# A Mamba, int8 MLP and MoE layer on one core: scans 2 to 4 regrouped to 4 states x 32 channels

## The chip, the core and the metric

The kernel runs on one core of a Trainium2 chip. The metric is the device time in microseconds. The engines are called as in the profile: PE (TensorE matmuls; PEld its weight loads), DVE (VectorE), ACT (ScalarE), POOL (GpSimd) and SP, whose queue issues most of the DMAs.

## What is computed

Four sequences (batches) of 512 tokens x 512 features pass through three sublayers with residuals. The one that matters here is a Mamba mixer:

```python
xz = einsum('ed,bld->bel', in_proj_weight, hidden_states)       # x: 1024 channels, z: 1024
x = silu(depthwise_conv4(x))
dt, Bc, Cc = split(x_proj_weight @ x, [128, 16, 16])
delta = softplus(dt_proj_weight @ dt + dt_proj_bias)
def step(h, (d_t, B_t, C_t, u_t)):                              # h: 1024 channels x 16 states
    h = h * exp(d_t[..., None] * A) + (d_t * u_t)[..., None] * B_t[:, None, :]
    y = einsum('bdn,bn->bd', h, C_t)
y = (ys + u * D) * silu(z)
out = out_proj_weight @ y
```

Then comes an int8 MLP ("smooth quant": two linear layers whose operands are scaled, rounded and clipped) and a mixture of 16 experts, top 2, with a shared expert beside it. Everything is float32 except the integer matmuls.

## The kernel before

**Stages.** `first()` prepares batch 0, `scan_stage(0)` scans it. Then for b = 1, 2, 3: `between(b, b-1)` projects batch b and runs the MLP of batch b-1, and `scan_stage(b)` scans batch b while it runs the experts of batch b-1. `last(3)` and `scan_stage(4, False, True)` finish batch 3. The change touches the three stages with b > 0, and what prepares them. The profiled scan stage of b = 2 is taken as the example: its units run from 815 to 1073 us of the span.

**A unit.** A scan stage has 128 units c = 16 j + n: block j of 128 channels, state n. For one unit ACT makes the decay `exp(delta[:, j] * A[n])` into one of three PSUM banks (`decay`, line 942), DVE runs the scan over 512 tokens (`scan_unit`, line 1277) and multiplies by the row C[n] (`product`, line 1289), and PE adds the products of a block into the bank Y with the identity as weights (`nsum`, lines 1870, 1876, 1881; line 1880 adds u x D once a block). POOL makes the inputs delta x u x B for two units at a time (`chunk`, line 663), and `du_block` once a block (line 651). Of 8 units POOL also multiplies one by C (line 718, unit 7 of 8, `on_pool`) and adds the products of two unit pairs (line 715), so that PE has 3 matmuls for 4 units. B and C stand spread over all 128 partitions in the tiles BB and CB (16 rows each), loaded by `broadcast`.

**Order.** Each engine's program is a loop over the unit number p, with the other work hung in at fixed p: an expert visit v begins at VISIT_AT[v] (8 shared visits every 4 units from p = 4, 23 routed ones every 3 units from p = 38) with `gate_up` on PE (line 1946), the tanh on ACT at +3, two DVE steps at +4 and +5 (lines 1304, 1311) and `down` on PE at +7 (line 1967 shared, 1975 routed). Four units ahead of a routed visit PE transposes its rows (line 1922). The output projection (`mixer_part`, line 2072) stands at p = 107 to 126. Engines are in order, so a late step holds all that is behind it on its engine.

**Softplus.** delta is made in steps; those of blocks 4 to 7 (line 1266 on DVE, 644 on POOL, inverses at line 915 on ACT) lie at the beginning of the scan stage, around p = 1.

**SP's queue** is in order too: a wait in it holds every DMA behind it. `load_up(w)` (line 442, 512 KB) waits for the gate_up of visit w-2 and `load_down(w)` (line 451, 256 KB) for the down of visit w-3. The loop `load_experts` issues load_up(w+2) and load_down(w+3) for w = 0 to 7, then waits for the scattered rows, then issues for each routed visit its down weights, rows (line 461), the store of finished rows and its up weights.

## Time and profile before

| | us |
|---|---|
| median of 3 runs | 1689.95 (1688.96 to 1692.02) |
| span of the profiled execution | 1684.0 |
| what lies around the span | 6.0 (median less span) |
| PE busy | 1428.3 (85%) |
| DVE busy | 1344.6 (80%) |
| ACT busy | 801.0 (48%) |
| POOL busy | 1060.6 (63%) |
| mean DMA | 150 GB/s, 252.13 MB |

How to read it: an engine's busy time is the union of its instructions. Matmuls are pipelined, so PE's busy time says how often it had something in hand, and its real pace is read from the distance between starts. A float32 matmul is two records (x2), with a weight load before each. The timeline gives start, duration and, in brackets, the idle time before and who ended it.

### The profile page before, as it was taken

How to read it: one execution, taken by the hardware profiler on the slowest of the kernel's cores; microseconds unless marked ns; L12 is line 12 of the kernel's file. 1: busy time of each engine (PE TensorE's matmuls, PEld its weight loads, DVE VectorE, ACT ScalarE, POOL GpSimd, SP SyncE). 2: the span in 40 equal slices, each digit the busy share in tenths (PEclk: the TensorE clock that was granted, in tenths of full speed). 3: DMA queues.
4: the chain of work that ended last, by engine and by line, in shares of the span. 5: the costliest groups of instructions: out<-in, count | busy, mean ns of one | idle time of the engine just before them, and what ended most of it. 6: DMA issues, size and time to landing. Idle time of an engine off the chain costs nothing.

```text
span 1684.0 us, 19335 instructions
## 1 busy us (share of the span) xinstructions
PE 1428.3 (85%) x5368; PEld 809.6 (48%) x5376; DVE 1344.6 (80%) x2215; ACT 801.0 (48%) x1374; POOL 1060.6 (63%) x684
## 2 busy tenths in 40 slices
PE   7588679999599899999599899999599999836994
PEld 4233224444365565444265565444265665324783
DVE  4588999676899999786899999796899999784212
ACT  3666444246634565246634565245734565222141
POOL 0399898103999899402999899501999999522101
PEclk9899899999799999999799999999799999968997
DMA  3550001403446673613535674612534773700984
GB/s 119 220 187 25 1 0 38 135 28 116 192 138 184 208 237 123 212 38 105 228 118 188 207 234 142 212 38 102 231 113 153 233 235 130 250 25 20 350 334 140
DMA packets 94073, 252.13 MB, mean 150 GB/s; under 512 B 11024, under 2 KB 11152, under 8 KB 88848
## 3 DMA queue, kind: packets, MB, share of 16 engines
q1 hardware_dynamic: 86688, 229.93, 40.3%
q0 software_dynamic: 5120, 16.78, 3.1%
q10 hardware_dynamic: 2160, 4.19, 0.6%
q8 instruction: 44, 0.72, 0.2%
q14 instruction: 61, 0.50, 0.1%
HBM read 207.87 MB, written 42.99 MB: 149 GB/s over the span
## 4 chain that ended last, share of the span: by engine, by line
PE 54%; DVE 17%; issue 12%; ACT 8%; POOL 7%; DMA 1%; DVEq 0%; POOLq 0%; SPq 0%; ACTq 0%
PE bank L1946 10%; PE bank L1804 7%; DVE bank L1277 5%; PE bank L2072 5%; PE bank L1817 5%; PE bank L1876 4%; PE bank L1881 4%; POOL work L663 4%; PE bank L1975 3%; PE bank L1870 3%; PE bank L1967 2%; PE bank L1922 2%; DVE work L1289 2%; DVE pairs L1289 2%; PE bank L1845 2%
## 5 line engine op out<-in xcount | busy, mean ns | idle before, releaser
L663 POOL TENSOR_TENSOR work<-du,BB 128x1024 f32<-128x1024 f32 x255 | 598.8, 2357 | 5.2 <-DVE work L1553 4.4
L942 ACT ACTIVATE bank<-delta,A_sb 128x512 f32<-128x512 f32 x512 | 349.9, 690 | 460.7 <-DVE pairs L1289 246.2
L1277 DVE TENSOR_TENSOR_SCAN bank<-bank,work 128x512 f32<-128x512 f32 x432 | 522.6, 1219 | 7.8 <-POOL work L663 4.0
L1946 PEld LDWEIGHTS bank<-x3T,ew_up 128*128 128x128 f32 x1488 | 215.7, 193 | 72.5 <-issue 63.7
L1946 PE MATMUL bank<-x3T,ew_up 128*128 128x128 f32 (+1 forms) x1488 | 235.8, 304 | 5.2 <-issue 5.2
L1289 DVE TENSOR_TENSOR pairs<-bank,CB 128x512 f32<-128x512 f32 x240 | 161.0, 671 | 3.9 <-PE bank L1881 2.9
L608 POOL TENSOR_TENSOR col<-col,halfpow 128x4 f32<-128x4 f32 (+1 forms) x8 | 7.8, 973 | 208.9 <-DVE col L1429 208.9
L1876 PE MATMUL bank<-pairs,ident 128*128 128x512 f32 x160 | 91.9, 659 | 43.7 <-DVE pairs L1289 16.6
L1289 DVE TENSOR_TENSOR work<-bank,CB 128x512 f32<-128x512 f32 x192 | 128.3, 668 | 0.0
L1817 PE MATMUL bank<-xT,wst 128*128 128x512 f32 x256 | 118.8, 610 | 9.2 <-DVE ew_up L1266 7.4
L2072 PE MATMUL bank<-wst,zg 128*128 128x512 f32 x256 | 117.0, 593 | 0.9 <-DVE zg L1297 0.9
L1804 PE MATMUL bank<-xT,wst 128*128 128x512 f32 x256 | 114.4, 593 | 0.7 <-ACT xT L829 0.7
L1241 DVE SCALAR_TENSOR_TENSOR u<-etm,cw,u 128x512 f32<-128x512 f32 x96 | 72.2, 752 | 40.6 <-ACT u L849 38.3
L1304 DVE SCALAR_TENSOR_TENSOR etm<-etm,bank 128x128 f32<-128x128 f32 (+1 forms) x124 | 38.6, 311 | 80.5 <-ACT etm L995 80.5
L1876 PE MATMUL bank<-work,ident 128*128 128x512 f32 x160 | 83.5, 604 | 12.5 <-POOL work L718 10.2
L715 POOL TENSOR_TENSOR work<-work 128x512 f32<-128x512 f32 x48 | 60.7, 1266 | 45.5 <-DVE work L1289 45.3
L1975 PE MATMUL bank<-ew_dn,etm 128*128 128x512 f32 x138 | 73.2, 612 | 18.2 <-ACT x3T L1009 17.9
L718 POOL TENSOR_TENSOR work<-work,CB 128x512 f32<-128x512 f32 x64 | 81.3, 1271 | 10.9 <-DVE work L1277 10.9
L1881 PE MATMUL bank<-pairs,ident 128*128 128x512 f32 x160 | 86.7, 625 | 0.0
L848 ACT COPY etm<-bank 128x512 f32<-128x512 f32 x32 | 18.8, 587 | 140.7 <-PE bank L1804 140.7
L1277 DVE TENSOR_TENSOR_SCAN work<-bank,work 128x512 f32<-128x512 f32 x64 | 77.5, 1211 | 8.8 <-PE bank L1881 6.3
L1817 PEld LDWEIGHTS bank<-xT,wst 128*128 128x128 f32 x256 | 49.3, 195 | 72.6 <-issue 59.2
(259 smaller groups left out, 2493.4 us busy)
## 6 DMA issues: line engine op xcount, KB each, us to landing
ew_up<-in_exp_w SPq DMA_DIRECT2D x93, 512.0 KB, 3.7
ew_dn<-in_exp_w SPq DMA_DIRECT2D x93, 256.0 KB, 4.3
hm<-xs_dram SPq DMA_DIRECT2D x69, 256.0 KB, 4.6
ys_dram<-x3T SPq DMA_DIRECT2D x69, 256.0 KB, 4.6
wst<-in_w_in SPq DMA_DIRECT2D x64, 256.0 KB, 2.7
BB<-bc_dram SPq DMA_DIRECT2D x16, 1024.0 KB, 7.7
CB<-bc_dram SPq DMA_DIRECT2D x16, 1024.0 KB, 9.7
wst<-in_out_w SPq DMA_DIRECT2D x32, 256.0 KB, 3.0
```

The lines of the kernel that those rows point to most:

```text
L663: nc.gpsimd.tensor_tensor(dBu[:, k % CHUNK_SLOTS, :, :], du[:, j % 2:j % 2 + 1, :].broadcast_to([P, 2, T]), BB[:, n0:n0 + 2, :], ALU.mult) ...
L718: nc.gpsimd.tensor_tensor(hi, hi, CB[:, (2 * m + 1) % NS, :], ALU.mult).then_inc(S["pool_prod"], 1)
L942: nc.scalar.activation(R[q % RING][:, :], delta[:, j, :], ACT.Exp, scale=A_sb[:, j, n:n + 1]).then_inc(S["da_ready"], 1)
L1277: V.tensor_tensor_scan(prod[c % (2 * PAIR_SLOTS)] if on_pool(q) else R[q % RING][:, :], R[q % RING][:, :], dBu[:, c // 2 % CHUNK_SLOTS, c ...
L1289: V.tensor_tensor(prod[c % (2 * PAIR_SLOTS)], R[q % RING][:, :], CB[:, n, :], ALU.mult).then_inc(S["prod_done"], 1)
L1804: ins = mm(ps[:, :], wst[:, slot, k * P:(k + 1) * P], xT[:, k, :], start=(k == 0), stop=(k == KD - 1))
L1817: ins = mm(z_bank(a, m)[:, :], wst[:, slot, k * P:(k + 1) * P], xT[:, k, :], start=(k == 0), stop=(k == KD - 1))
L1876: mm(Y[:, :], ident[:], prod[2 * (m % PAIR_SLOTS)], start=(m % (NS // 2) == 0), stop=False)
L1881: mm(Y[:, :], ident[:], prod[2 * (m % PAIR_SLOTS) + 1], start=False, stop=(m % (NS // 2) == NS // 2 - 1)).then_inc(S["nsum_done"], 1)
L1946: ins = mm(gu_bank(v)[:, part * n:(part + 1) * n], w[:, part * D + k * P:part * D + (k + 1) * P], rhs, start=(k == 0), stop=(k == KD - 1))
L1975: mm(down_ps[1][:, :], eT[:, v % 2, 0:P], w, start=True, stop=True).then_inc(S["down_done"], 1)
L2072: ins = mm(acc[t][:, :], zg[:, k, t * P:(t + 1) * P], wst[:, W_POS["o", m, k] % W_RING, :], start=(k == 0), stop=(k == NBLK - 1))
```

## The change

In the scans of b = 1, 2, 3 a unit is no longer one state of 128 channels but 4 states of 32 channels: partition 32 s + i holds state s of a group and channel 32 q + i, with c = 16 j + 4 g + q (state group g, quarter q of the block's channels). Batch 0 stays as it was, with the states in another order in the weights.

- B and C need 4 tiles each (Brep, Crep, filled by `spread_rows`: 8 DMAs of 256 KB) and no longer 16.
- delta and delta x u of a block must stand four times, once for each state of a group. `replicate(b, j)` writes both to DRAM (2 stores of 256 KB), waits until these have landed, and loads them back into drep and durep in 8 DMAs of 256 KB. The decay reads drep, the chunk reads Brep and durep.
- The sum over the states of a partition group is made by PE: `quad_sum(g)` has four matmuls for four units, with a 128 x 32 matrix `fold` as weights, each into 32 partitions of Y (tile_position (0, 32 q)). The pair sums on POOL are gone.
- POOL makes 2 of 8 products with C (units 3 and 7), DVE 6; before it was 1 and 7.
- Products have 16 slots and no longer 8.
- The visits of the scan stages begin at p = 9, every 3.25 units for the shared ones and from p = 39 every 3 for the routed; the first down moves from p = 12 to 17. The router's steps move by 2 to 5 units, the scatters are at 2 a step. In the last stage all stays.
- The `lost` steps, products and subtractions of the softplus of blocks 4 to 7 move into the unit loop (DVE p = 0, 1 and 6, 7; POOL k = 7, 8), as do ACT's second row norm, inverses and the copies to x3T.
- The loads of the next MLP's weights change their place: guT and gu at the end of the stage wait for the last chunk and the last product.

```diff
+QUADS = UNITS // 4
+SLOTS = 16
+GROUPS = 4
+ROWS = P // GROUPS
...
+STAGE = Order(visits=tuple(9 + 13 * v // 4 for v in range(SHARED)) + tuple(39 + 3 * r for r in range(ROUTED)),
+              norm=1, inverses=3, x3=5, logits=7, logits_copy=9, route=10, rank=14, place=15, first_down=17,
+              gate_sums=10, gates=19, gate_weights=14, scatter=11, scatters=2)
...
+LOST_AT = {4: 0, 5: 0, 6: 1, 7: 1}
+ERROR_AT = {4: 6, 5: 6, 6: 7, 7: 7}
+LESS_AT = {4: 7, 5: 7, 6: 8, 7: 8}
...
-    return q % 8 in ((3, 7) if q < UNITS else (7,))
+    return q % 8 in (3, 7)
...
+REPLICATE_BEFORE = {j: min(i for i in range(3, ROUTED + 3) if STAGE.visits[SHARED + i - 3] >= NS * (j - 1))
+                    for j in range(4, NBLK)}
...
+            def replicate(b, j):
+
+                n = NBLK * (b - 1) + j
+                sp.wait_ge(S["delta_ready"], NBLK * b + j + 1)
+                sp.dma_start(rep_dram[j], delta[:, j, :]).then_inc(S["rep_out"], 16)
+                sp.wait_ge(S["du_ready"], NBLK * b + j + 1)
+                sp.dma_start(rep_dram[NBLK + j], du[:, j % 2, :]).then_inc(S["rep_out"], 16)
...
+                    sp.wait_ge(S["da_ready"], UNITS * b + NS * (j - 1))
+                    sp.wait_ge(S["dbu_ready"], PAIRS * b + NS // 2 * (j - 1))
+                sp.wait_ge(delta_in, replicas(b, j))
+                sp.wait_ge(du_in, replicas(b, j))
+                sp.wait_ge(S["rep_out"], 32 * (n + 1))
+                for src, dst, landed in ((rep_dram[NBLK + j], durep[j % 2], du_in), (rep_dram[j], drep[j % 2], delta_in)):
+                    for g in range(GROUPS):
+                        sp.dma_start(dst[g * ROWS:(g + 1) * ROWS, :, :],
+                                     src.rearrange("(q i) t -> i q t", q=GROUPS)).then_inc(landed, 16)
...
                     if w + DOWN_RING < SHARED:
                         load_down(be, w + DOWN_RING)
+                    if w == 3:
+                        replicate(be + 1, 2)
+                replicate(be + 1, 3)
                 sp.wait_ge(S["scattered"], 16 * 2 * TT * (be + 1))
...
                 for j in range(ROUTED + 6):
+                    for i in range(4, NBLK):
+                        if REPLICATE_BEFORE[i] == j:
+                            replicate(be + 1, i)
...
-                    broadcast(b, 0)
+                    spread_rows(b)
                     weights("z", b, 4, NBLK)
-                    wait(sp, "lin_ps", 2 * TT * b)
-                    broadcast(b, 1)
+                    replicate(b, 0)
+                    replicate(b, 1)
                     weights("o", b, 0, 4)
...
+                    nc.gpsimd.tensor_tensor(
+                        dBu[:, k % CHUNK_SLOTS, :, :], Brep[:, g:g + 1, :].broadcast_to([P, 2, T]),
+                        durep[j % 2][:, q0:q0 + 2, :], ALU.mult).then_inc(S["dbu_ready"], 1)
...
-                    for i in range(4):
+                    for i in range(2):
                         softplus_lost(a, i)
-                    softplus_less(a, 0)
-                    du_block(a, 0)
-                    chunk(a, 0)
-                    for i in range(1, 4):
                         softplus_less(a, i)
+                        du_block(a, i)
                 if m is not None:
                     norm(2 * m + 1)
                 if a is not None:
+                    chunk(a, 0)
+                    for i in range(2, 4):
+                        softplus_lost(a, i)
+                        softplus_less(a, i)
                     for i in range(4, 8):
                         softplus_sum(a, i)
...
+                src = delta[:, j, :] if b == 0 else drep[j % 2][:, n % GROUPS, :]
+                nc.scalar.activation(R[q % RING][:, :], src, ACT.Exp, scale=(A_first if b == 0 else A_sb)[:, j, n:n + 1]
...
-                for i in range(4, 8):
-                    lost(a, i)
...
+                def quad_sum(g):
...
+                    pe.wait_ge(S["prod_done"], dve_products(UNITS * b + 4 * g + 4))
+                    pe.wait_ge(S["pool_prod"], pool_products(UNITS * b + 4 * g + 4))
+                    if part == GROUPS - 1:
+                        pe.wait_ge(S["skip_ready"], NBLK * b + j + 1)
+                        mm(Y[:, :], skip_diag(b, j), u[:, j, :], start=False, stop=False)
+                    for q in range(GROUPS):
+                        ins = mm(Y[q * ROWS:(q + 1) * ROWS, :], fold[:], slot(b, 4 * g + q), start=(part == 0),
+                                 stop=(part == GROUPS - 1), tile_position=(0, q * ROWS))
+                    ins.then_inc(S["nsum_done"], 1)
```

## Rows read from the trace of the kernel before

**Rows 1.** Windows of stage 2: window, length, busy time (instructions), PEclk, DMA share, GB/s

```profile
core 0: us, PE busy (x) PEld busy (x) DVE busy (x) ACT busy (x) POOL busy (x), PEclk, DMA share, GB/s
828.00:890.00 62.00, 56.75 (x203) 36.69 (x204) 60.49 (x107) 23.41 (x41) 59.77 (x40) 0.97 0.31 107
890.00:1030.00 140.00, 129.87 (x631) 85.30 (x630) 135.84 (x200) 78.17 (x146) 128.77 (x75) 0.99 0.70 215
1030.00:1082.00 52.00, 51.58 (x145) 24.47 (x144) 43.91 (x57) 20.28 (x35) 41.44 (x27) 1.00 0.48 167
```

**Rows 2.** Timeline of DVE in mid-stage, back to back: start, us, engine, line, operation

```profile
914.19 1.22 DVE L1277 TENSOR_TENSOR_SCAN bank<-bank,work 128x512 f32<-128x512 f32 x1
915.32 0.67 DVE L1289 TENSOR_TENSOR pairs<-bank,CB 128x512 f32<-128x512 f32 x1
915.91 1.22 DVE L1277 TENSOR_TENSOR_SCAN bank<-bank,work 128x512 f32<-128x512 f32 x1
```

**Rows 3.** Timeline of DVE: units 0 and 1, softplus, then units 2, 8, 32, 40, 104

```profile
815.37 2.33 DVE L1277 TENSOR_TENSOR_SCAN bank<-bank,work 128x512 f32<-128x512 f32 x2
820.27 6.79 DVE L1266 TENSOR_TENSOR work<-pairs,work 128x512 f32<-128x512 f32 x4 [2.57 <-ACT work L915]
827.80 1.22 DVE L1277 TENSOR_TENSOR_SCAN bank<-bank,work 128x512 f32<-128x512 f32 x1
...
840.13 1.22 DVE L1277 TENSOR_TENSOR_SCAN bank<-bank,work 128x512 f32<-128x512 f32 x1
...
890.18 1.23 DVE L1277 TENSOR_TENSOR_SCAN bank<-bank,work 128x512 f32<-128x512 f32 x1 [0.60 <-POOL work L663]
...
906.21 2.34 DVE L1277 TENSOR_TENSOR_SCAN bank<-bank,work 128x512 f32<-128x512 f32 x2
...
1029.78 2.34 DVE L1277 TENSOR_TENSOR_SCAN bank<-bank,work 128x512 f32<-128x512 f32 x2
```

**Rows 4.** Timeline of PE in the shared visits, back to back

```profile
880.11 1.02 PE L1870 MATMUL bank<-work,ident 128*128 128x512 f32 x2
880.97 1.88 PE L1967 MATMUL bank<-ew_dn,etm 128*128 128x512 f32 x4
882.69 1.02 PE L1876 MATMUL bank<-work,ident 128*128 128x512 f32 x2
...
884.41 3.62 PE L1946 MATMUL bank<-x3T,ew_up 128*128 128x256 f32 x16
887.86 1.02 PE L1870 MATMUL bank<-pairs,ident 128*128 128x512 f32 x2
```

**Rows 5.** Timeline of PE: a matmul with 32-column weights between ones with 128

```profile
748.29 1.04 PE L1844 MATMUL bank<-u,xpw 128*32 128x512 f32 x2
749.27 1.12 PE L1845 MATMUL bank<-u,xpw 128*128 128x512 f32 x2
750.23 3.60 PE L1817 MATMUL bank<-xT,wst 128*128 128x512 f32 x8
```

**Rows 6.** Costliest groups of the page: busy us, mean ns

```profile
L718 POOL TENSOR_TENSOR work<-work,CB 128x512 f32<-128x512 f32 x64 | 81.3, 1271 | 10.9 <-DVE work L1277 10.9
```

**Rows 7.** Timeline of SP: one issue of a broadcast, one of expert weights (visit 7)

```profile
803.20 0.44 SPq L423 DMA_DIRECT2D BB<-bc_dram  x1
...
883.26 0.46 SPq L442 DMA_DIRECT2D ew_up<-in_exp_w  x1
```

**Rows 8.** Chain that ended last: start, us, a 256 KB load, a 256 KB store

```profile
893.98 2.84 DMA hm<-xs_dram
...
1663.19 2.01 DMA ys_dram<-zg
```

**Rows 9.** DMA view of 800 to 812 us, all 16 engines busy

```profile
DMA packets 1098, 4.93 MB, mean 411 GB/s; under 512 B 112, under 2 KB 112, under 8 KB 624
```

**Rows 10.** Timelines around the start and the end of stage 2: POOL, ACT, PE

```profile
804.70 1.27 POOL L651 TENSOR_TENSOR du<-delta,u 128x512 f32<-128x512 f32 x1
810.01 1.90 ACT L942 ACTIVATE bank<-delta,A_sb 128x512 f32<-128x512 f32 x3
...
1081.36 3.60 PE L1804 MATMUL bank<-xT,wst 128*128 128x512 f32 x8
```

More of the change, by code:

```diff
@@ L9 @@
 from contextlib import ExitStack
+from dataclasses import dataclass
 import numpy as np
@@ L299, in rows_bank, with slot @@
             return bank[1] if r < 2 else bank[0]
+        def slot(b, c):
+            return prod[c % (2 * PAIR_SLOTS)] if b == 0 else slots[c % SLOTS]
         def width(v):
```

364 lines of the change are left out of this document (232 added, 132 removed).

## Prediction

> **What bounds the kernel now.** I read the chain that ended last first: PE has 54% of it, DVE 17%. Then the stages: the timeline shows three scan stages of equal shape, 382 us apart, so I work out stage 2 and take it three times. In windows of that stage [rows 1] three engines are full at once: from 828 to 890 us DVE has 60.5 of 62 us, POOL 59.8, PE 56.8; to 1030 us DVE has 135.8 of 140; in the last 52 us PE has 51.6 and DVE only 43.9. The timelines say who leads. In mid-stage DVE's starts touch: 1.13 us from a scan to what follows, 0.59 from a product to the next scan [rows 2]. A group of 8 units costs DVE 8 x 1.13 + 7 x 0.59 = 13.2 us before any expert work, and 123.6 us pass from unit 40 to unit 104 [rows 3], 15.4 us for 8. In the shared visits PE touches too: 0.86 us for a matmul of the sum, 1.72 for a down, 3.45 for a gate_up [rows 4]; 8 units hold two visits (10.3) and six sums (5.2), 15.5 us. At the end the last product is done at about 1072.3, but PE begins the next stage at 1081.4 [rows 10]: there it is 9 us behind DVE. So a microsecond taken from DVE counts between units 40 and 104, one taken from PE in the head and in the tail.
>
> **The parts.** The sum is made against the span of 1684.0; the median is 6.0 above it, and I add the change to the median.
>
> (a) *DVE.* One product of 8 goes to POOL: 16 a stage x 0.59 = 9.4 us [rows 2]. Units 40 to 104 are half of them: **-4.7**. In the head PE and the loads set the pace (below), in the tail PE does: nothing there. POOL loses 32 pair sums and gains 16 products, all of about 1.27 us [rows 6]: 20 us less work, so it no longer holds DVE.
>
> (b) *PE's sum.* Three matmuls for four units (3 x 0.86 = 2.58 us) become four with 32 columns of weights. A float32 matmul is two records of 0.43 us. The trace has 32-column matmuls among wide ones: start to start 0.98 and then 0.96 us where 0.86 is the rate [rows 5], so entering and leaving costs 0.11 each, 0.22 a group. What it doesn't have is four of them into four different column groups. The bounds: all in a row, 4 x 0.86 + 0.22 = 3.66 us; all four at once, 0.86 + 0.22 = 1.08. I take the middle case: starts keep their order and the second record of a matmul needs the columns of its first, so only the second record of one and the first of the next can overlap: 5 records, 2.15 + 0.22 = **2.37** a group. Against 2.58 that is 0.21 less for each of six groups in the tail: **-1.3**. In the middle PE isn't the limit: 2.67 visits (3.1 us each, 8.3), two groups (4.7) and a skip matmul (0.4) are 13.4 us for 8 units, under DVE's 13.9.
>
> (c) *The way into the stage.* Scan 0 now starts at 815.4 [rows 3]. The decay at 810.0 [rows 10] will need drep: du of block 0 is done at about 802 (its instruction is at 804.7 now [rows 10], and two of the four 1.25 us `lost` steps ahead of it go). Two stores land 0.8 + 2.5 us later (2.01 for one [rows 8]), eight issues take 8 x 0.45 us [rows 7], and 2.1 MB at 411 GB/s [rows 9] take 5.1 us after 2.2 us of latency (2.84 less the bytes of rows 8). That gives 813 to 814 for drep and 815.5 for scan 0: nothing lost. Scan 2 stands at 827.8 behind a wait and the 6.8 us of softplus products [rows 3]. After, chunk 1 is queued on POOL behind four sums (about 826.5), and the softplus products come at p = 6 and 7, under no wait; six units x 1.57 (13.2 less 0.59, by 8) and 5.4 to 6.8 us give 841 to 843 for unit 8, now 840.1: **+1**, up to +3.
>
> (d) *SP's queue in the shared visits.* This is the largest term. `replicate(b, 2)` stands after load_down(6), which waits for the down of visit 3, at p = 25. PE needs from visit 0 (845 us) five gate_ups, four downs, four groups and the ranks: 17.3 + 6.9 + 9.5 + 2.7, so 881; DVE alone would be there at 876. I take 880. Stores to 883.3, eight issues to 887, and only then load_up(6), whose 0.5 MB lies behind 2.1 MB: 883.3 + 2.2 + 2.6 MB / 411 GB/s = 892. Its gate_up stands at p = 28; the tanh at p = 31 gives it one unit of grace, to 887. Queued behind it: on PE the group sums and the down of visit 4, on ACT (behind the tanh) every decay, and behind these DVE; the 16 product slots don't help, since ACT waits. **+5**. load_down(7) then waits for that down (898), load_up(7) lands near 902, and the tanh at p = 34 comes 3 us late: **+3**. `replicate(b, 3)` precedes the rows of visit 0 (issued at 907, landed near 911, needed by p = 37 at 911): 0 to +2. Now load_up(7) is issued at 883.3 [rows 7] and nothing waits for it.
>
> (e) *Blocks 4 to 7* have their replicas between routed visits. SP arrives at p = 46, is held until p = 50, and rows and up weights land at p = 53 and 54, just when needed. The DMA share is 0.70 there [rows 1], and 2.6 MB per 16 units (30 us) add 87 GB/s to 215. **+2** for the stage, 0 to +8.
>
> (f) *Batch 0, the last stage, the constants:* one 64 KB load more, one 0.3 us reduction; 0. The later loads of guT and gu end at about 1070 and 1081; their users come at 1075 and after 1100: 0, covered by PE's tail. If PE's tail shrinks by over 5 us, guT is the next to be late.
>
> Sum for a stage: -4.7 - 1.3 + 1 + 5 + 3 + 2 = **+5**. Three stages: +15, so 1689.95 + 15 = **1705**.
>
> **A rule of the skill.** Rows 5 show a 32-column matmul at the full price of a wide one, plus 0.11 us at each switch. The Trainium skill, page "TensorE: Matmul & The Clock Gate", section "Part 3: Packing small matmuls", says that matmuls into different column groups run together, four in little more than the time of one. No row here has two such neighbours. By that rule a group would take 1.08 us, which is rival 2. The page "TensorEngine Tiling (Array Packing)", section "Key Properties", says that a change of tiling mode drains the array; on that the trace agrees, with 0.11 us.
>
> **Rivals.**
>
> 1. *The four matmuls run one after another* (3.66 us a group). For it: PE has 5 to 8% free in a stage [rows 1], and this asks 32 x 1.08 = 35 us more of it. Against my forecast it costs 1.29 us a group: head +7 (six groups, part under the late loads), middle 16.0 us for 8 units in place of DVE's 13.9 to 15, +9, tail six groups, +8. +24 a stage: 1777. Chance 0.14.
>
> 2. *All four at once* (1.08 us). The tail falls by 6 x 1.29 = 7.7 of the 9 us that PE is behind there, the head by 1: 1705 - 3 x 8.7 = 1679. Chance 0.12.
>
> 3. *SP's queue isn't in the way* (the other side). The stores land, and 2.1 MB arrive, before visit 6 needs its weights. It decides at a lateness of 0 in (d): load_up(6) must land by 887, 5 us earlier than I have it, which needs PE to reach the down of visit 3 at 876 and a quick return of the stores. Then (d) and (e) are 0 and a stage is 1 - 4.7 - 1.3 = -5: 1675. Chance 0.22; together with rival 2, 1649, chance 0.05.
>
> 4. *The replicas load at half rate.* Each load writes only 32 partitions, while every large load of this trace writes 128, so 411 GB/s may not hold. If half, each is 5 us later: about +4 at scan 0, at visit 6 and at the first rows: 1705 + 3 x 12 = 1741. Chance 0.15.
>
> 5. *The change doesn't do what it says*: POOL makes its second product too late for PE. POOL's 8 units are now 4 chunks (2.36) and 2 products (1.27), 12.0 us, under 13.9; I give it nothing.
>
> **The numbers.** The forecast has a chance of 0.32. Low end 1662 (leaves out most of the case at 1649, and some of the optimistic tails), high end 1760 (leaves out rival 1 and a little of rival 4). A measurement of this kernel tells about 0.2% (3.4 us) from no change. Faster: rival 3, its joint case and two thirds of rival 2, 0.35. Within 0.2%: parts of rival 2 and of the forecast's lower edge, 0.08. Slower: 0.57.
>
> **What would show it.** (a) Units 40 to 104 in 119 us or so, with POOL idle between its chunks. (b) The distance between two wide matmuls around a group: 2.4, 1.1 or 3.7 us. (c) Scan 0 within 2 us of 815.4 less the shift of the stage. (d) PE idle 5 to 10 us before the gate_up of visit 6, released by a DMA into ew_up, and again at visit 7; SP's eight issues 3 us after its stores. (e) Short waits for hm and ew_up once in 16 units. The forecast is wrong if PE doesn't wait in the shared visits, or if the group takes over 3 us.

## The result, and the profile after

| | before | after |
|---|---|---|
| median, us | 1689.45 (4 runs, 1686.75 to 1692.02) | 1900.62 (4 runs, 1892.71 to 1901.97) |
| ratio | | 1.1236 (95%: 1.1207 to 1.1264) |
| span of the profiled execution, us | 1684.0 | 1900.2 |

The changed kernel is 211 us slower: the direction was forecast, the size (15 us, at most 70) was not. The page of after, its busy times, DMA totals and chain:

```profile
span 1900.2 us, 19981 instructions
PE 1372.2 (72%) x5568; PEld 751.4 (40%) x5568; DVE 1316.5 (69%) x2169; ACT 798.1 (42%) x1375; POOL 1002.0 (53%) x636
DMA packets 126477, 296.30 MB, mean 156 GB/s; under 512 B 14880, under 2 KB 15136, under 8 KB 123552
...
PE 40%; DMA 17%; POOL 12%; DVE 10%; issue 9%; SPq 7%; ACT 4%; POOLq 0%; DVEq 0%; ACTq 0%
```

Every engine is busy for less time than before, and still the span is longer: the time went into waits. DMA and SP's queue, 1% of the chain before, hold 24% of it now. Of the example stage (b = 2), the lines that answer to [rows 3], and PE's turn to the next stage, which answers to [rows 10]:

```profile
894.48 1.23 DVE L1436 TENSOR_TENSOR_SCAN bank<-bank,work 128x512 f32<-128x512 f32 x1
...
905.92 1.23 DVE L1436 TENSOR_TENSOR_SCAN bank<-bank,work 128x512 f32<-128x512 f32 x1 [4.15 <-POOL work L779]
...
989.03 1.23 DVE L1436 TENSOR_TENSOR_SCAN bank<-bank,work 128x512 f32<-128x512 f32 x1 [6.74 <-ACT bank L1072]
...
1022.59 1.22 DVE L1436 TENSOR_TENSOR_SCAN bank<-bank,work 128x512 f32<-128x512 f32 x1
...
1164.34 1.22 DVE L1436 TENSOR_TENSOR_SCAN bank<-bank,work 128x512 f32<-128x512 f32 x1
...
1220.01 1.55 PE L1962 MATMUL bank<-xT,wst 128*128 128x512 f32 x3
```

These are units 0, 2, 32, 40 and 104. With the start of the stage's preparation (the first input projection of batch b, at 699.2 us in before and 768.9 us in after) they give a table of one period:

| stretch | before | after | more |
|---|---|---|---|
| input projection to unit 0 | 116.2 | 125.6 | 9.4 |
| unit 0 to 40 (shared visits) | 90.8 | 128.1 | 37.3 |
| unit 40 to 104 | 123.6 | 141.8 | 18.2 |
| unit 104 to the next input projection | 51.6 | 55.7 | 4.1 |
| a period | 382.1 | 451.1 | 69 |

Three periods make 207 of the 211 us, so the stage is again the thing to explain, and the head of it above all. The windows of the same stretches as [rows 1], units 2 to 32, 32 to 104, and the tail:

```profile
905.90:989.00 83.10, 52.96 (x206) 30.32 (x206) 65.02 (x107) 28.00 (x51) 62.13 (x42) 0.79 0.36 104
989.00:1164.30 175.30, 122.20 (x664) 76.84 (x664) 130.41 (x189) 76.74 (x143) 116.53 (x62) 0.86 0.78 229
1164.30:1220.00 55.70, 47.61 (x184) 21.60 (x184) 42.46 (x55) 21.39 (x37) 31.98 (x19) 0.88 0.57 185
```

DVE, which had 60.5 of 62 us and 135.8 of 140 [rows 1], now has 65.0 of 83.1 and 130.4 of 175.3. Nobody is full. The last three numbers of a row are PE's granted clock (as a share of the full one), the DMA share and GB/s: before, the clock was between 0.97 and 1.00, and after, it is between 0.79 and 0.88, and the DMA engines are busy 78% of the middle with hardly more GB/s than at 70% before (229 against 215).

**The order of a replica in SP's queue.** SP's timeline (issues only), replica 2 and the beginning of replica 3:

```profile
971.87 0.43 SPq L497 DMA_DIRECT2D rep_dram<-delta  x1
972.35 0.44 SPq L499 DMA_DIRECT2D rep_dram<-du  x1
976.49 1.74 SPq L513 DMA_DIRECT2D CB<-rep_dram  x4
978.27 1.86 SPq L513 DMA_DIRECT2D BB<-rep_dram  x4
```

and the chain of waits (start, length, what) over a replica of the shared visits and one of the routed ones:

```profile
972.35 4.07 DMA rep_dram<-du
...
980.17 9.31 DMA ew_up<-in_exp_w
989.53 3.78 PE bank L2115 x8
...
1080.42 4.82 DMA rep_dram<-du
...
1090.21 8.48 DMA hm<-xs_dram
1098.73 1.12 PE bank L2091 x4
```

Here ew_up is an expert's up weights and hm are the rows gathered for it. One replica is on the chain with all it has: the store's way out (4.1 to 5.7 us), eight issues, and then the load of an expert that stands behind 2 MB, 8.5 to 9.3 us where the page of before has medians of 3.7 (ew_up) and 4.6 (hm). PE sees it as one wait. Its timeline at visits 6 and 7, behind replica 2:

```profile
989.53 3.78 PE L2115 MATMUL bank<-x3T,ew_up 128*128 128x256 f32 x8 [13.61 <-DMA ew_up<-in_exp_w]
...
1000.51 3.14 PE L2115 MATMUL bank<-x3T,ew_up 128*128 128x256 f32 x8 [3.17 <-DMA ew_up<-in_exp_w]
```

Behind such a wait PE runs at the lower clock level. PE's timeline, first the float32 sum after a wait of 9.87 us, then the same instruction 7 us later:

```profile
1098.73 1.12 PE L2091 MATMUL bank<-ident,hm 128*128 128x128 f32 x4 [9.87 <-DMA hm<-xs_dram]
1099.78 1.94 PE L2049 MATMUL bank<-CB,fold 128*32 128x512 f32 x8
1101.64 2.08 PE L2115 MATMUL bank<-x3T,ew_up 128*128 128x128 f32 x8
...
1106.73 1.06 PE L2049 MATMUL bank<-BB,fold 128*32 128x512 f32 x8
1107.73 1.12 PE L2144 MATMUL bank<-ew_dn,etm 128*128 128x512 f32 x2
```

**The rate of a replica.** DMA view of after, 977 to 987 us, the replica's loads (GB/s in 40 slices, then the total, then the share of the 16 engines):

```profile
GB/s 0 49 238 279 385 312 246 188 221 172 221 172 238 254 189 229 205 197 197 197 188 205 229 254 180 229 197 213 180 197 197 213 229 221 213 229 180 221 188 229
DMA packets 1136, 2.10 MB, mean 210 GB/s; under 512 B 117, under 2 KB 117, under 8 KB 1136
...
q1 hardware_dynamic: 1136, 2.10, 101.6%
```

All sixteen engines are busy throughout, and move 210 GB/s where [rows 9] have 411. The two stretches differ in more than the target, though: a replica's packets have 2 KB, and those of [rows 9] 4.5 KB in the mean (4.93 MB in 1098).

### The profile page after: what moved, and what is told of

Same layout as the page of the kernel before. It is cut to its first block, busy times and chain, and to the rows that moved or that the text cites. A ratio compares the mean times of both kernels' runs of the same rounds, so it can differ in the third digit from the quotient of the medians.

```text
span 1900.2 us, 19981 instructions
## 1 busy us (share of the span) xinstructions
PE 1372.2 (72%) x5568; PEld 751.4 (40%) x5568; DVE 1316.5 (69%) x2169; ACT 798.1 (42%) x1375; POOL 1002.0 (53%) x636
## 4 chain that ended last, share of the span: by engine, by line
PE 40%; DMA 17%; POOL 12%; DVE 10%; issue 9%; SPq 7%; ACT 4%; POOLq 0%; DVEq 0%; ACTq 0%
PE bank L2115 11%; DMA ew_up<-in_exp_w 7%; PE bank L1962 6%; PE bank L2245 4%; POOL work L772 4%; DMA rep_dram<-du 4%; SPq L513 3%; PE bank L2144 3%; PE bank L2049 3%; DMA hm<-xs_dram 3%; PE bank L2136 2%; DVE bank L1436 2%; POOL delta L735 2%; PE bank L1975 2%; POOL work L779 2%
## 5 line engine op out<-in xcount | busy, mean ns | idle before, releaser
L1436 DVE TENSOR_TENSOR_SCAN bank<-bank,work 128x512 f32<-128x512 f32 x384 | 461.8, 1218 | 96.0 <-ACT bank L1072 82.4
L779 POOL TENSOR_TENSOR work<-BB,CB 128x1024 f32<-128x1024 f32 x192 | 453.7, 2377 | 95.0 <-DVE bank L1436 59.6
L1072 ACT ACTIVATE bank<-BB,A_sb 128x512 f32<-128x512 f32 x384 | 261.4, 689 | 347.6 <-DVE BB L1443 114.5
L2115 PE MATMUL bank<-x3T,ew_up 128*128 128x128 f32 (+1 forms) x1488 | 275.9, 336 | 83.1 <-DMA ew_up<-in_exp_w 82.1
L2091 PE MATMUL bank<-ident,hm 128*128 128x128 f32 x276 | 50.1, 311 | 145.4 <-DMA hm<-xs_dram 128.5
L772 POOL TENSOR_TENSOR work<-du,BB 128x1024 f32<-128x1024 f32 x63 | 148.3, 2388 | 4.4 <-DVE work L1711 4.4
L1072 ACT ACTIVATE bank<-delta,x3T 128x512 f32<-128x512 f32 x128 | 86.3, 688 | 103.9 <-DVE work L1443 53.3
L735 POOL TENSOR_TENSOR delta<-delta,x3T 128x512 f32<-128x512 f32 x26 | 40.4, 1584 | 126.2 <-ACT x3T L1036 126.2
L834 POOL TENSOR_TENSOR pairs<-pairs,CB 128x512 f32<-128x512 f32 x40 | 51.3, 1281 | 71.0 <-DVE pairs L1436 71.0
L1443 DVE TENSOR_TENSOR pairs<-bank,CB 128x512 f32<-128x512 f32 x120 | 80.2, 668 | 2.8 <-issue 2.3
```

Of the source, the lines that this page charges most:

```text
L735: nc.gpsimd.tensor_tensor(delta[:, m, :], delta[:, m, :], sp_ln(a, m), ALU.add).then_inc(S["sum_ready"], 1)
L772: nc.gpsimd.tensor_tensor(dBu[:, k % CHUNK_SLOTS, :, :], du[:, j % 2:j % 2 + 1, :].broadcast_to([P, 2, T]), BB[:, n0:n0 + 2, :], ALU.mult) ...
L779: nc.gpsimd.tensor_tensor(dBu[:, k % CHUNK_SLOTS, :, :], Brep[:, g:g + 1, :].broadcast_to([P, 2, T]), durep[j % 2][:, q0:q0 + 2, :], ALU.m ...
L1072: nc.scalar.activation(R[q % RING][:, :], src, ACT.Exp, scale=(A_first if b == 0 else A_sb)[:, j, n:n + 1]).then_inc(S["da_ready"], 1)
L1436: V.tensor_tensor_scan(slot(b, c) if on_pool(q) else R[q % RING][:, :], R[q % RING][:, :], dBu[:, c // 2 % CHUNK_SLOTS, c % 2, :], 0.0, AL ...
L1443: V.tensor_tensor(slot(b, c), R[q % RING][:, :], c_row(c), ALU.mult).then_inc(S["prod_done"], 1)
```

## The experiments

My theory after reading the two traces (A): the stage waits for replicas 2 to 7 in SP's queue, since each holds the experts' loads behind it by the return of its stores, its issues and its bytes. Rival B: the bytes themselves cost it, wherever they are issued. Rival C: the sums or the products (PE, POOL, DVE) are slower than priced. To these came three questions of detail: the store's return or the burst, what halves the rate, and what the order of work at the start of the stage costs. Times are compared with the 1900.6 of after, or with the version that they edit. All versions but e10 and e16 were run once; the four runs of after lie between 1892.7 and 1902.0, so the steps of 17 to 26 us below (e4, e14, e8, e6) are clear of that spread, but each rests on one run.

### Without replicas, with the sums in a row

`e1_no_replicas` leaves replicas 2 to 7 away:

```diff
+                if j >= 2:
+                    return
+                n = 2 * (b - 1) + j
```

> The changed kernel without the replicas of blocks 2 to 7 (their two stores, the wait for them and their eight loads; decays and chunks of these blocks read what blocks 0 and 1 left, so the scans' results are wrong). Theory A and B (the replicas' DMAs cost the time, by the order of SP's queue or by their volume): the four groups of 8 units that now take 22 to 25 us go to the 14.1 of their neighbours, 4 x 9.7 us a stage, and the shared visits lose about 17: 1900 - 3 x 56 = 1730. Theory C (the regrouped work on the engines, or the new order of the head, costs it): above 1850.

Measured: 1719.3. So 181 of the 211 us hang on six replicas a stage; 30 are something else. Eight units in mid-stage take 13.5 to 14.9 us, once 16.5, where part (a) of the prediction had 13.9. Units 0 and 40 of stage 2 and unit 0 of stage 3 in this run, and that last one in after:

```profile
834.94 1.23 DVE L1438 TENSOR_TENSOR_SCAN bank<-bank,work 128x512 f32<-128x512 f32 x1
...
938.25 1.22 DVE L1438 TENSOR_TENSOR_SCAN bank<-bank,work 128x512 f32<-128x512 f32 x1
...
1225.24 1.23 DVE L1438 TENSOR_TENSOR_SCAN bank<-bank,work 128x512 f32<-128x512 f32 x1
```

```profile
1346.68 1.23 DVE L1436 TENSOR_TENSOR_SCAN bank<-bank,work 128x512 f32<-128x512 f32 x1 [0.15 <-ACT bank L1072]
```

Unit 0 to 40 takes 103.3 us, and 128.1 in after: replicas 2 and 3 cost 24.8 us a stage. Unit 40 to the next unit 0 takes 287.0, and 324.1 in after: replicas 4 to 7 cost 37.1.

`e3_wide_sums` makes the four matmuls of a sum with the 128 x 128 identity, so that they can't run together:

```diff
-                        ins = mm(Y[q * ROWS:(q + 1) * ROWS, :], fold[:], slot(b, 4 * g + q), start=(part == 0),
-                                 stop=(part == GROUPS - 1), tile_position=(0, q * ROWS))
+                        ins = mm(Y[:, :], ident[:], slot(b, 4 * g + q), start=(part == 0 and q == 0),
+                                 stop=(part == GROUPS - 1 and q == GROUPS - 1))
```

> The four matmuls of a sum with the identity as weights, 128 columns wide, one after another, in place of the four 32-column ones side by side (the sum over the states of a group is then left out, results wrong). A group goes from 1.0 to about 3.43 us on PE, 2.4 x 32 = 78 us a stage. If PE's relief is what shortens the tail (from 51.6 to 31.1 us behind unit 104): 15 us more there, and some more elsewhere, in sum 1900 + 3 x 20 = 1960. If PE's sum never mattered: 1900.

Measured: 2019.3, 119 us more, twice the 60 that I expected. PE's timeline of it, and of after:

```profile
1109.54 3.71 PE L2049 MATMUL bank<-CB,ident 128*128 128x512 f32 x8
1113.09 0.60 PE L2091 MATMUL bank<-ident,hm 128*128 128x128 f32 x4
```

```profile
1037.20 1.06 PE L2049 MATMUL bank<-pairs,fold 128*32 128x512 f32 x8
1038.20 1.16 PE L2115 MATMUL bank<-x3T,ew_up 128*128 128x128 f32 x8
```

3.55 us from start to start against 1.00. The four column groups do run together, float32 and all, so C falls for the sums. 96 groups x 2.55 us are 245 us of PE; 119 of them show.

### What of a replica costs the time

`e2_no_return_wait`: the loads of blocks 2 to 7 read block 0's copy and don't wait for their own stores.

```diff
-                sp.wait_ge(S["rep_out"], 32 * (n + 1))
+                if j < 2:
+                    sp.wait_ge(S["rep_out"], 32 * (n + 1))
+                o = j if j < 2 else 0
```

> Stores and loads of blocks 2 to 7 all stay, but the loads read the DRAM copy of block 0, so that SP doesn't wait for the store of the same block to land (wrong results for these blocks). Theory A1 (SP standing still for 4 to 6 us at each replica is most of it): 5 us x 6 x 3 = 90 less, about 1810. Theory A2 (the 2.1 MB that stand in front of the next expert loads are most of it): at most 15 us less, 1885 or more. Half and half: about 1850.

Measured: 1865.6, 35 less, between the two theories. 18 replicas x 4.1 to 5.7 us of return would be 73 to 103. The run doesn't take the return out alone: the loads now share the engines with their own stores, and the page's medians from issue to landing rise from 4.5 and 7.6 to 6.3 and 8.8 us, so 35 is a lower bound of what the return costs. At most 146 of the 181 are then the issues and the burst; how these divide isn't shown.

`h1_before_traffic` is the kernel *before* with nothing but the traffic: the same stores, the wait and eight 256 KB copies within DRAM, at the same places of SP's queue.

```diff
+                sp.wait_ge(S["rep_out"], 160 * n + 32)
+                for i in range(8):
+                    sp.dma_start(far_dram[i], rep_dram[j + NBLK * (i < 4)]).then_inc(S["rep_out"], 16)
```

> The kernel before, with the replicas' DMAs of blocks 2 to 7 added at the same places of SP's queue: two stores of 256 KB (delta and u of the block), the wait for them, eight copies of 256 KB of these (DRAM to DRAM, so nothing reads them). Nothing else of the change. If SP's order and the bytes alone cost the time: 25 us a stage in the shared visits and 4 x 9 in the routed ones, 1690 + 3 x 50 = 1840, 1780 at least. If the loss needs the regrouped scan (its decays and chunks wait for the replicas): within 30 us of 1690.

Measured: 1806.3, 119 more than before. The layout of units has no part in that: a kernel with the old scans, sums and visits loses 119 us to this traffic at this place. It stays under the 181; these copies write no SBUF, and nothing in this kernel waits for them. Why it is less isn't shown.

`e5_act_queue` moves replicas 2 to 7 to ACT's queue, the loads one at each unit, so that no wait of theirs stands before an expert's load. (It contains the order of `e4_pool_order` below, and makes du of a block one block earlier.)

```diff
+                            if p == NS * (j - 2) + 6:
+                                rep_stores(j)
+                            if 0 <= p - NS * (j - 1) - 1 < 2 * GROUPS:
+                                rep_load(j, p - NS * (j - 1) - 1)
```

> e4 with the replicas of blocks 2 to 7 moved from SP's queue to ACT's: the same stores and loads, the same bytes, issued by ACT in the unit loop (stores at unit 16(j-2)+6, the eight loads one a unit from 16(j-1)+1, so that the wait for the stores is met), and du of a block made one block earlier. Theory A (the order in SP's queue: expert loads stand behind the wait and the 2.1 MB): the groups of 22 to 25 us go to 14 or 15 and visit 6's wait is gone, 1883 - 3 x 50 = 1730, down to 1700. Theory B (the volume: 296 MB are too much beside the experts' loads): the waits for ew_up and hm stay, 1830 or more.

Measured: 1765.9, 118 less than with the replicas in SP's queue (1883.5), and less of a gain than expected (1730). The bytes are the same and still go onto 32 partitions, so B can't have more than what is left. But the edit changed three things at once, the queue, the spacing of the loads and how early the stores go out; no run separates them. PE's wait for rows in the whole run falls from 128.5 us to 5.8, that for up weights rises from 82.1 to 109.4.

### The start of the stage, and the first weights

`e4_pool_order` puts POOL's `lost(2)` and `lost(3)` ahead of the norm and of chunk 0:

```diff
+                    for i in range(2, 4):
+                        softplus_lost(a, i)
                 if m is not None:
                     norm(2 * m + 1)
```

> One part undone: POOL makes the error products of blocks 2 and 3 before the norm and before chunk 0, which waits for the first replica. If that order is what made ACT wait 10.1 us in front of the relus of blocks 6 and 7 (scan 0 starts 9.4 us later in its period): 3 x 9 less, 1873. If the landing of the first replica sets the start anyway: 1895 to 1900.

Measured: 1883.5, 17 less, where I expected 27. The lines of after that led to it are POOL's and ACT's timelines:

```profile
882.34 2.34 POOL L779 TENSOR_TENSOR work<-BB,CB 128x1024 f32<-128x1024 f32 x1 [3.63 <-DMA CB<-rep_dram]
884.63 1.26 POOL L742 TENSOR_TENSOR work<-pairs,work 128x512 f32<-128x512 f32 x1
```

```profile
885.99 0.69 ACT L1002 ACTIVATE pairs<-bank,dtb 128x512 f32<-128x512 f32 x1 [10.10 <-POOL work L742]
```

Chunk 0 waits for replica 0, `lost(2)` stands behind it in POOL's order, and ACT's activations of the softplus wait for `lost(2)`: three engines are strung on the first replica, by an order that looks harmless.

`e6_up_first` issues each load_up one step ahead of load_down, which waits for the first down (now at p = 17):

```diff
+                load_up(be, UP_RING)
                 for w in range(SHARED):
-                    if w + UP_RING < SHARED:
-                        load_up(be, w + UP_RING)
+                    if w + UP_RING + 1 < SHARED:
+                        load_up(be, w + UP_RING + 1)
```

> e5 with the up weights of the shared visits issued one step ahead of the down weights in SP's queue (load_up(3) no longer behind load_down(3), which waits for the first down at p = 17). If the order of SP's queue is also what makes units 8 to 24 take 20 and 25 us in place of 18 and 16: 3 x 8 to 3 x 12 less than e5. If the later first down itself or PE's work does it: within 5 us of e5.

Measured: 1740.3, 26 less, within what was expected.

`e8_spread_loads` spreads a replica's loads over eleven units in place of eight:

```diff
+REP_STEPS = (1, 2, 4, 5, 7, 8, 10, 11)
```

> e6 with the eight loads of a replica spread over 11 units in place of 8. If what is left are short bursts that meet the experts' loads: 3 x 2 to 3 x 5 us less than e6, about 1730. If it is the mean volume: within 3 us of e6 (1740).

Measured: 1720.2, 20 less, more than the 6 to 15 expected. `e9_free_replicas` has both repaired orders and no replicas 2 to 7, and `e9b_one_on_pool` takes POOL's second product of 8 back:

```diff
-    return q % 8 in (3, 7)
+    return q % 8 in ((3, 7) if q < UNITS else (7,))
```

> The changed kernel with both repairs of order (POOL's list before the stage, up weights ahead of down weights) and without the replicas of blocks 2 to 7 (wrong results for these): what the regrouped scan would give if its copies were free. From e1 (1719), e4 (-17) and e6 over e5 (-26): 1676. If the regrouped scan has its own cost in the head that no order mends: 1690 or more.

> e9 with POOL making 1 of 8 products with C and DVE 7, as before the change. The prediction's part (a): 0.59 us x 16 more on DVE a stage, all of it on the path where DVE sets the pace (units 24 to 127 here): 3 x 7.7 = +23 against e9. If DVE isn't the limit: within 5.

Measured: 1675.6 and 1696.6. With free replicas the change is worth 12 to 14 us against before (1687.2 beside it, 1689.45 in the median), and POOL's second product alone 21. So all the gain is that product: without it the new scans, sums and orders are 7 to 9 us slower than before, even with the replicas free. What the regrouping does is to take the pair sums from POOL, which makes room for the product. C falls: neither sums nor products lose the 211. And 45 us lay still between 1720 and 1676.

### What halves the rate

`e11_wide_loads` (the changed kernel) and `e10_spread_wide` (e8) load one quarter onto all 128 partitions where four quarters went onto 32:

```diff
-                        sp.dma_start(dst[g * ROWS:(g + 1) * ROWS, :, :],
-                                     src.rearrange("(q i) t -> i q t", q=GROUPS)).then_inc(landed, 16)
+                        sp.dma_start(dst[:, g, :],
+                                     src[g * ROWS:(g + 1) * ROWS, :].partition_broadcast(GROUPS)).then_inc(landed, 16)
```

> The changed kernel with one edit: a replica's eight loads have the same source rows, the same 2 MB and the same places in SP's queue, but each writes one quarter of the replica on all 128 partitions (32 rows of DRAM read four times over), where each wrote four quarters on 32 partitions. Theory N (a load that lands on 32 partitions gets about 210 GB/s from sixteen busy engines, one that lands on 128 gets about 400): the eight loads take 5 us where they took 10, the up weights behind them land in 5 to 6 us instead of 8.5 to 9.3, and the wait of the queue's next expert falls by about 5 us for each of replicas 2 to 7: 1870, range 1850 to 1885, and the DMA view of the stretch after a replica's first load shows 350 GB/s or more. Theory M (the rate is a matter of packets of 2 KB read back from DRAM, or of a row that is read four times, whatever it is written to): 210 GB/s stays, and 1895 to 1905.

> The kernel with the repaired orders, replicas 2 to 7 in ACT's queue and their loads spread over eleven units (1720), with the wide loads of the run beside it. With free replicas these orders gave 1676, so 45 us are left between the two. Theory N: most of the 45 is experts' weights that share the engines with half-rate loads; at the full rate the same bytes cost at most half of it: 1695, range 1685 to 1708. Theory M: no change, 1715 to 1725. At 1680 or less the replicas would have been free of cost, and the kernel faster than the one before, which neither expects.

Measured: 2194.8 and 2043.5 (ratio to before 1.2079, 1.2031 to 1.2128), both far off either theory. DMA view of e11, 974 to 987 us:

```profile
GB/s 0 0 0 50 0 50 0 101 101 101 101 101 82 95 76 95 82 82 95 101 76 82 95 76 101 76 101 82 95 76 101 76 82 95 101 76 95 82 82 95
...
q1 hardware_dynamic: 496, 0.99, 23.9%
```

About a quarter of the sixteen engines is busy, at 76 to 101 GB/s, or by an estimate from that 19 to 25 GB/s for each of four. The source's outermost axis is the repeat, with four entries. The Trainium skill has it (page "DMA: Bandwidth & Descriptors", section "Rules for kernel authors": a leading zero-stride repeat of c copies confines a transfer to at most c engines), and the trace agrees. So my test had changed two things, and told nothing certain of the 32 partitions; though 25 GB/s for an engine, against 13 in after (210 by sixteen), was a hint.

`e12_block_to_128` and `e15_spread_full_rate` change the written partitions; the source rows, bytes, packet size and the sixteen engines stay (only the order in which the rows are read changes with them):

```diff
+                        sp.dma_start(dst[:, g, :], src).then_inc(landed, 16)
```

> The changed kernel with one edit: each of a replica's eight loads reads the same 256 KB of DRAM as before, but writes it to one quarter of the replica on all 128 partitions in the block's own order (so the replica's data are not the ones that the scan wants: this run leaves the replication out and keeps its traffic). Before it, the loads that read 32 rows four times over and wrote 128 partitions had shown 25% of the engines busy at 90 to 100 GB/s, that is 4 of the 16: the outermost axis had four entries. So that run could not tell whether the 32 partitions halve the rate. Theory N (they do: 210 GB/s with all 16 engines busy where the rows of other loads show 411): here the eight loads take 5 to 6 us, the DMA view of that stretch shows 380 GB/s or more, the up weights behind them land in 5 to 6 us, and the time is 1870, range 1850 to 1885. Theory M (reading back from DRAM, packets of 2 KB): 210 GB/s and 1895 to 1905.

> The kernel with the repaired orders, replicas 2 to 7 in ACT's queue and their loads spread over eleven units (1720), with loads of the same 256 KB to 128 partitions (the replication is left out, its traffic kept). Free replicas gave 1676 in these orders, so 45 us lie between. Theory N: most of it is experts' weights sharing engines with half-rate loads; at the full rate at most half is left: 1695, range 1685 to 1705. Rival: it is the stores' and loads' bytes and the bursts as such, whatever their rate: 1712 to 1725.

Measured: 1835.7 and 1677.1, 65 and 43 less than their originals, more than I had expected. DMA view of e12, 974 to 979 us:

```profile
GB/s 0 0 0 0 0 0 82 115 180 295 377 426 410 377 426 442 344 442 262 164 180 213 197 279 295 279 229 164 279 279 377 328 426 426 393 410 393 410 377 459
```

Slices of 377 to 459 GB/s, in turn with slower ones. Over six us of replica 2's burst (953.8 to 959.8 us, 2.05 MB) the mean is 341 GB/s, under the 380 that theory N asked, and from the first load's issue to the landing of the up weights behind it 9.8 us pass, where after has 13.0. The page's median from issue to landing falls from 7.6 to 4.8 us for drep (in BB) and from 4.5 to 3.5 for durep (in CB). The first two lines are of after, the last two of e12:

```profile
CB<-rep_dram SPq DMA_DIRECT2D x96, 256.0 KB, 4.5
BB<-rep_dram SPq DMA_DIRECT2D x96, 256.0 KB, 7.6
```

```profile
CB<-rep_dram SPq DMA_DIRECT2D x96, 256.0 KB, 3.5
BB<-rep_dram SPq DMA_DIRECT2D x96, 256.0 KB, 4.8
```

Theory M is out, and theory N stands in the main: the 32 partitions cost a good third of the rate, 210 against 341 GB/s. The rest of the way to the 411 of [rows 9] isn't theirs. The Trainium skill, page "SBUF — State Buffer", section "Door 1: The DMA port swizzle", gives 8 of 16 ports and 189 GB/s, measured at 1 MiB, for partitions 0 to 31 (all 16 for 0 to 127); the 210 of this trace are near that.

What the rate buys shows in two waits of the whole run: in e8 PE waits 51.0 us for up weights and ACT's decays 43.3 us for replicas, in e15 23.2 and 13.7. And e15, with all the replicas' bytes, is 1.5 us above e9, which has none of replicas 2 to 7: spread and at the full rate the bytes cost nothing that one run could show, and B falls.

`e14_port_order` asks whether neighbouring loads can share the two halves of the partitions:

```diff
-                    for g in range(GROUPS):
+                    for g in (0, 2, 1, 3):
```

> The changed kernel with the four loads of each half replica in the order of partitions 0, 64, 32, 96 instead of 0, 32, 64, 96, same data. If partitions 0 to 63 and 64 to 127 are reached by different halves of the path into SBUF, neighbouring loads could overlap and the 2 MB go faster than 210 GB/s: theory P expects 300 GB/s or more and 1875 to 1885. Theory Q (each engine takes the loads one after the other and all are at the same one at a time): 210 GB/s and 1895 to 1905. I hold Q for likelier, since the loads of one queue were seen to go one after the other.

Measured: 1883.4, 17 less; the rate is 225 GB/s (970.5 to 980.5 us, the window that answers to the one with 210). P was right on the time and wrong on the rate; why 7% of rate are worth 17 us isn't shown.

### The change with its transfers repaired

`e16_states_inside` is e8 with partition 4i + g for channel i and state group g in place of 32g + i. The load has 32 rows as its outermost axis, each four times, and lands on all partitions. `e17_layout_only` has the same edit in the changed kernel's own queue. (In both, B and C are spread in the same way, by an edit of `spread_rows` that isn't printed here.)

```diff
-                        sp.dma_start(dst[g * ROWS:(g + 1) * ROWS, :, :],
-                                     src.rearrange("(q i) t -> i q t", q=GROUPS)).then_inc(landed, 16)
+                        sp.dma_start(dst[:, g, :],
+                                     src[g * ROWS:(g + 1) * ROWS, :].unsqueeze(1).broadcast_to([ROWS, GROUPS, T])
+                                     ).then_inc(landed, 16)
...
-            V.tensor_reduce(fold[:], ident.rearrange("p (q i) -> p i q", q=GROUPS), AX.X, ALU.add).then_inc(S["init"], 1)
+            V.tensor_reduce(fold[:], ident.rearrange("p (i q) -> p i q", q=GROUPS), AX.X, ALU.add).then_inc(S["init"], 1)
...
-    grouped = al.reshape(NBLK, GROUPS, ROWS, NS // GROUPS, GROUPS).transpose(4, 2, 0, 3, 1).reshape(P, NBLK, NS)
+    grouped = al.reshape(NBLK, GROUPS, ROWS, NS // GROUPS, GROUPS).transpose(2, 4, 0, 3, 1).reshape(P, NBLK, NS)
```

> The version with the repaired orders, replicas 2 to 7 in ACT's queue and spread loads (1720), with one change of layout: partition 4i + g holds channel i and state group g, where it was 32g + i. A replica's load then writes one quarter on all 128 partitions from 32 rows, each read four times, with the rows as the outermost axis (32 entries, so all 16 engines), and nothing of the computation is left out. The same traffic to 128 partitions without the replication had given 1677. Expected 1678, range 1670 to 1688, against 1689 of the kernel before: 0.2 to 1.0% faster. If reading one row four times has a price of its own, the loads show less than 380 GB/s and the time is 1690 to 1715.

> The changed kernel with that change of layout alone: queues, orders and places as they were. The traffic to 128 partitions without the replication gave 1836 there. Expected 1836, range 1825 to 1848; what stays above 1690 is then the queue and the orders, not the rate.

Measured: e16 1679.06 (9 runs) against 1688.68 for before (14 runs), ratio 0.9951 (0.9927 to 0.9975): the whole computation, and 0.5% faster than before. e17 1859.6, 41 less than after but 24 more than e12, and outside the range expected. Two things differ between their traces. Four issues of the repeated load take SP 2.5 us against 1.7 to 1.9 for e12's, 1.4 us more for a replica; 18 x 1.4 = 25 us would be the 24. And the loads run at 305 GB/s (964.5 to 972.5 us) against 341. No run tests either. The windows of e16, units 2 to 33 and 33 to 105:

```profile
824.50:898.30 73.80, 59.36 (x236) 35.00 (x236) 66.55 (x110) 29.41 (x53) 61.97 (x42) 0.82 0.49 165
898.30:1028.70 130.40, 108.63 (x657) 69.62 (x657) 129.68 (x190) 77.38 (x145) 116.43 (x62) 0.96 0.88 309
```

DVE has 129.7 of 130.4 us in the middle: it is the bound again, as part (a) assumed. From unit 32 to 104 exactly, 130.6 us pass, 9.0 fewer than the 139.6 of before. The DMA engines move 309 GB/s, 80 more than in after. What PE waits for in the whole run, the numbers behind the last bar: for up weights 82.1 us in after and 18.4 in e16, for the rows hm 128.5 in after, PE's largest wait, and none in e16. Up weights in after and e16, then rows in after and e16:

```profile
L2115 PE MATMUL bank<-x3T,ew_up 128*128 128x128 f32 (+1 forms) x1488 | 275.9, 336 | 83.1 <-DMA ew_up<-in_exp_w 82.1
```

```profile
L2143 PE MATMUL bank<-x3T,ew_up 128*128 128x128 f32 (+1 forms) x1488 | 253.2, 317 | 26.3 <-DMA ew_up<-in_exp_w 18.4
```

```profile
L2091 PE MATMUL bank<-ident,hm 128*128 128x128 f32 x276 | 50.1, 311 | 145.4 <-DMA hm<-xs_dram 128.5
```

```profile
L2119 PE MATMUL bank<-ident,hm 128*128 128x128 f32 x276 | 44.0, 284 | 24.5 <-ACT x3T L1125 20.1 <-DVE x L1501 4.5
```

The head stays longer than before: units 2 to 32 take 72.3 us against 62.4. In e9, where replicas 2 to 7 are free, they take 69.8, so 7 of the 10 us aren't theirs. The new order of visits and softplus is what is left to blame; no run tests it.

**The account.** One version after the other: after 1900.6; POOL's order -17; replicas out of SP's queue and spaced -118; up weights first -26; loads spread -20; full rate -41; 1679.1. The sizes hold in this order: the layout alone had -41 at either end, the others were not tried in another order.

## Why the prediction was wrong

**The steps that failed.** Parts (d) and (e), which price the replicas in SP's queue. The sum had +8 us a stage for replica 2, nothing for replica 3 and +2 for replicas 4 to 7. After against e1 shows 24.8 for replicas 2 and 3 and 37.1 for 4 to 7. To these come the late load_up(3), about 8.5 us a stage (e6), and the late start, 9.4 us, where (c) had found nothing lost at unit 0; the engines' gain of some 10 us takes part of it back. The mechanism of (d) was seen, its size wasn't; (e) had the wrong path, since it compared mean rates and left the queue out.

**What bounds the kernel.** Right for before, and it carried over to what the engines do; wrong as a picture of after, where transfers bound the stage.

**(a) DVE, -4.7 a stage.** Right in mechanism: stretches between replicas run at 14.1 to 14.9 us for 8 units where I had 13.9, and e16's middle is 9.0 us shorter. Between units 40 and 104 the size was right too: the second product is worth 4.3 us there (119.9 us in e9b, 115.6 in e9). But in three stages it is worth 21 us, where the term gave 14; outside the middle I had counted nothing.

**(b) The sum, 2.37 us a group.** Wrong by 1.37: it is 1.00. I took the middle of my two bounds by an argument on the order of records that no row supported. The bound of 1.08, rival 2, was the right price. By that the trace agrees with the Trainium skill, page "TensorE: Matmul & The Clock Gate", section "Part 3: Packing small matmuls": 1.00 us for the four, 0.86 for a wide one. In after, where PE waits for DMAs, the saving can't be seen; that the sums matter shows in e3, where four in a row cost 119.

**(c) The way into the stage, +1.** Unit 0 comes 9.4 us later. I followed the replica itself and found it on time, and did not follow what I had listed as moved: `lost(2)` and `lost(3)` behind chunk 0 on POOL, and ACT's activations behind them. The prediction names the queue of POOL only for unit 2 and unit 8. That coupling cost 17 us (e4), about 6 of the 9.4 us of each stage; the rest stays open. From unit 0 to unit 8 the stage takes 27.8 us where it took 24.8, inside the +1 to +3 of the term.

**(d) SP's queue in the shared visits, +5 +3.** The mechanism is the one named, at the place named: PE waits for ew_up after replica 2's eight issues. The sizes are not: PE waited 13.6 us before visit 6, where I looked for 5 to 10, and 3.2 at visit 7. The stores took 4.1 to 5.7 us to return where I had 2.5 to 3.3, from a single store under little traffic [rows 8]; the 2 MB took 10 us, not 5 (rival 4); the up weights took 9.3 us from issue to landing. And I gave each wait its lateness alone. DVE waits 6.74 us for the decay of unit 32, and after a wait PE works at the lower clock level, 1.86 us for a sum of 1.00; that this makes the next visit late as well is likely, but no run isolates it. The second miss in (d) is load_up(3), which stands behind the load_down that waits for the first down: the diff moves that down from p = 12 to 17, I carried it through to load_up(6) and never to load_up(3). That is 26 us (e6). With the late start it would make up some 18 of the 22 us by which SP came to replica 2 after my 880: at 971.9, which is 902.2 on the clock of before (after's stage begins 69.7 us later).

**(e) Blocks 4 to 7, +2 for four replicas.** This was the weakest step and the largest miss: I priced them by mean GB/s and found room. Behind each of them PE waits 8.5 to 10.9 us for rows (8.50 at 1055.99, 9.87 at 1098.73, 10.88 at 1134.67, 9.59 at 1170.87), and the stretch of 40 to 104 plus the tail is 22.3 us longer where (a) should have made it 4.7 shorter. A mean of 215 GB/s says nothing about a burst of 2 MB in a queue with loads that, by my own working, would land just when needed. It is also the term whose upper bound (+8) was too small: that bound had no row behind it.

**(f)** No line of after speaks against 0.

**Rivals.** The conditions of 2 and 4 both came true, which I had priced one by one (1679 and 1741); together they would give 1715, so neither is the miss. Those of 1 and 3 failed. Rival 4's 12 us for a stage counted three replicas of eight; the rate is worth 41 us (e16, e17) to 65 (e12) in three stages, not 36.

**The range.** It ended at 1760 since each case was priced as the sum of separate latenesses. The error was in common to all of them: a replica that stands in an in-order queue ahead of loads that are due. h1 shows 119 us of it without anything else of the change.

## What to carry to other kernels

When a change puts a group of transfers into a queue that feeds a just-in-time stream, price every group by the whole of it, return of the store, issues, bytes at the rate of *their* shape, against the slack of the next transfer behind it, and multiply by the number of groups; a mean bandwidth with room in it proves nothing. Put such transfers in another queue, spread them, and let them land on all 128 partitions with many entries on the outermost axis (32 rows had all sixteen engines at work here, 4 repeats a quarter of them). List every instruction that moved behind the new wait on every engine, since the ones that look unrelated (a softplus step, a down weight) are the ones that are missed.

## What the runs showed of the hardware

- Four float32 matmuls with 128 x 32 weights into the four column groups take 1.00 us from start to start (after), where one wide matmul takes 0.86 [rows 4] and four in a row took 3.55 (e3).
- 256 KB loads onto 32 partitions run at 210 GB/s with all 16 DMA engines busy; onto 128 partitions, with packets of the same size, it was 341 GB/s over six us of a burst (e12), with slices up to 459. Loads whose source has a repeat of 4 outermost use a quarter of the engines, at 76 to 101 GB/s (e11).
- Two 256 KB stores to DRAM land 4.1 to 5.7 us after the second is issued under load, against 2.0 for one in [rows 8].
- One issue of a load with each row repeated four times takes SP 0.6 us (e17), against 0.44 for a plain one [rows 7].
- After a wait of 8 to 10 us PE works at the lower of its two clock levels for a while: the sum took 1.86 us, then 1.00 seven microseconds later. The mean clock of units 2 to 32 was 0.79, against 0.97 before.
